# Slots of single columns, two light degrees ranked last, and a reordered attention setup in a graph-and-experts kernel

## What is computed

```
x = x + gat(layernorm(x), src, dst, W, att_src, att_dst, bias)        # attention over each node's incoming edges, 8 heads
x = x + experts(layernorm(x))                                         # each node goes through one of 32 experts, 256 -> 64 -> 256
x = x + relations(layernorm(x), weight[16], edge_weight, edge_type)   # out[dst] += (x[src] @ weight[type]) * edge_weight
x = x + two_experts(layernorm(x))                                     # two of 8 experts, the same two for all nodes, 256 -> 512 -> 256
```

## Time and profile before

| | us |
|---|---|
| median of three runs | 3556.42 (3555.38 to 3558.89) |
| the profiled execution | 3553.55 |
| its span | 3551.9 |
| busy PE / DVE / POOL / ACT | 2038.9 / 1808.5 / 1954.4 / 757.0 |
| stages, from the trace: search and ranking | 0 to 293.8 |
| attention, experts, relation products | 293.8 to 2012.6 |
| relations | 2012.6 to about 3078 |
| choose two, feed-forward | 3078 to 3551.9 |

### The profile page before, as it was taken

How to read it: one execution, slowest core, us unless ns; L and a number is a source line. 1 busy time by engine, 2 the same in 40 slices (tenths; PEclk the granted TensorE clock), 3 DMA queues, 4 the chain that set the end, 5 groups by cost and what they waited for, 6 DMA issues and landing times. The chain is left out here.

```text
span 3551.9 us, 37123 instructions
## 1 busy us (share of the span) xinstructions
PE 2038.9 (57%) x7510; PEld 1302.1 (37%) x7510; DVE 1808.5 (51%) x4035; ACT 757.0 (21%) x1428; POOL 1954.4 (55%) x1920
## 2 busy tenths in 40 slices
PE   1600399999999999999979500000000000369996
PEld 1400266565666656666546200000000000346664
DVE  7643765555556666566530254544454444314545
ACT  3200133333333333333223200000000000013331
POOL 5434874455655767777710277777777777300111
PEclk9955699999999999999989855555555555579998
DMA  6536344445555555554522533333333333100000
GB/s 237 212 102 179 86 126 136 142 135 155 144 146 152 146 166 149 168 165 143 150 87 76 173 106 106 105 106 105 106 105 105 105 105 105 45 30 12 18 18 25
DMA packets 209182, 416.09 MB, mean 117 GB/s; under 512 B 53562, under 2 KB 96018, under 8 KB 208930
## 3 DMA queue, kind: packets, MB, share of 16 engines
q0 software_dynamic: 87168, 239.28, 25.3%
q1 hardware_dynamic: 114706, 167.99, 13.3%
q10 hardware_dynamic: 7056, 6.63, 0.5%
HBM read 259.06 MB, written 154.68 MB: 116 GB/s over the span
## 5 line engine op out<-in xcount | busy, mean ns | idle before, releaser
L822 POOL DMA_INDIRECT gat_rows<-h_table,gat_idx x824 | 923.2, 1120 | 468.8 <-issue 246.0
L1412 POOL DMA_INDIRECT rel_rows<-transformed,rel_idx x824 | 779.1, 945 | 258.2 <-issue 258.2
L1042 PE MATMUL bank<-tr_wr,tr_xt 128*128 128x512 f32 x1568 | 725.1, 602 | 33.8 <-ACT tr_row L913 28.9
L1584 PE MATMUL bank<-weight,rec 128*128 128x1 f32 x196 | 42.0, 352 | 1073.0 <-DVE weight L1610 1073.0
L1584 PEld LDWEIGHTS bank<-weight,rec 128*128 128x128 f32 x196 | 41.9, 333 | 1073.8 <-DVE weight L1610 1073.8
L1009 PE MATMUL bank<-mo_xt,mo_w 128*128 128x256 f32 (+1 forms) x1600 | 429.1, 392 | 1.6 <-ACT mo_ones L894 1.6
L1487 DVE SCALAR_TENSOR_TENSOR bank<-rel_rows,rel_now,bank 128x256 f32<-128x256 f32 x823 | 403.1, 490 | 51.6 <-DVE bank L1487 27.0
L1042 PEld LDWEIGHTS bank<-tr_wr,tr_xt 128*128 128x128 f32 x1568 | 294.4, 192 | 322.9 <-issue 276.4
L913 ACT ACTIVATE tr_row<-bank 128x512 f32<-128x512 f32 x392 | 233.7, 597 | 678.1 <-PE bank L1042 665.5
L1027 PE MATMUL bank<-mo_w,mo_ht 128*128 128x256 f32 x1568 | 366.7, 380 | 0.0
L1009 PEld LDWEIGHTS bank<-mo_xt,mo_w 128*128 128x128 f32 x1600 | 286.3, 192 | 133.0 <-issue 101.2
(11 more groups left out here) (274 smaller groups left out, 2034.7 us busy)
## 6 DMA issues: line engine op xcount, KB each, us to landing
transformed<-tr_row SPq DMA_DIRECT2D x392, 256.0 KB, 2.4
windows<-win SPq DMA_DIRECT2D x34, 736.0 KB, 3.2
gat_rows<-h_table,gat_idx POOLq DMA_INDIRECT x824
rel_rows<-transformed,rel_idx POOLq DMA_INDIRECT x824, 2.8
h_table<-hrow ACTq DMA_DIRECT2D x49, 132.0 KB, 2.1
xa<-x SPq DMA_DIRECT2D x1, 6272.0 KB, 23.9
rec<-x_moved SPq DMA_DIRECT2D x1, 6272.0 KB
tr_x<-records SPq DMA_DIRECT2D x24, 256.0 KB, 4.1
```

Source lines behind the costliest of these rows:

```text
L822: pool.indirect_dma_start(out=rows[:, column(u, j), :], out_offset=None, in_=p.h_table[:], in_offset=bass.IndirectOffsetOnAxis(ap=idx[u][: ...
L1042: ins = pe.matmul(p.bank[6 + c % 2][:], xt2[:, k, u * P:(u + 1) * P], wr[:, k, m * CW:(m + 1) * CW], start=(k == 0), stop=(k == KD - 1))
L1412: pool.indirect_dma_start(out=rows[b][:, j, :], out_offset=None, in_=p.transformed[:], in_offset=bass.IndirectOffsetOnAxis(ap=idx[b][:, j: ...
```

## The change

There are four parts. (1) Ranking: the bins are no longer min(degree, 63). Degrees 0 to 8 keep their bins, degrees 9 and 10 get bins 62 and 63, and all above move down by two, so the order of the nodes is rising in degree but for those with 9 and 10, which come last. DVE computes that with four small operations instead of one. (2) `COLS1` is 8 columns and then 1 at a time: 25 slots instead of 13. The same code computes the counts from it (the shift becomes one by 0 bits). (3) ScalarE clears `rows` instead of DVE, with a copy scaled by 0; POOL waits for it (`cleared`) behind `tables`, and DVE waits for it before its tile loop. (4) In DVE's setup the block of windows and `tables` stands ahead of the fill of `score`, the masks and the expert setup with its wait for `set_turned`.

```diff
-COLS1 = [8] + [2] * (WIN // 2 - 4)
+COLS1 = [8] + [1] * (WIN - 8)
+LAST_DEGREES = N_EDGES // N_NODES * 5 // 8 - 1, N_EDGES // N_NODES * 5 // 8
...
-            chain(dve.tensor_scalar(bin_[:], xa[:, :, C_DEG], float(DBINS - 1), None, ALU.min))
+            lo_last, hi_last = LAST_DEGREES
+            apart = hi_last - lo_last + 1
+            chain(dve.tensor_scalar(bin_[:], xa[:, :, C_DEG], float(lo_last), float(DBINS - 1 - hi_last), ALU.is_ge, ALU.mult))
+            chain(dve.scalar_tensor_tensor(bin_[:], xa[:, :, C_DEG], float(DBINS - 1), bin_[:], ALU.min, ALU.add))
+            chain(dve.tensor_scalar(rank[:], xa[:, :, C_DEG], float(hi_last + 1), float(hi_last + 1 - DBINS - apart), ALU.is_ge, ALU.mult))
+            chain(dve.tensor_tensor(bin_[:], bin_[:], rank[:], ALU.add))
...
             pool.wait_ge(tables, 1)
+            pool.wait_ge(cleared, 1)
...
         @block.scalar
         def _(act):
+            act.activation(rows[:], p.ones[:, 0:1].unsqueeze(2).broadcast_to([P, WIDTH, HT]), ACT.Copy, scale=0.0).then_inc(cleared, 1)
             act.wait_ge(tables, 1)
...
             chain(dve.tensor_copy(p.tails[:], row[:, 2, :]))
-            chain(dve.memset(rows[:], 0.0))
-            chain(dve.memset(score[:], LOWEST))
-            chain(dve.tensor_copy(identb[:], p.ident[:]))
-            dve.tensor_scalar(other[:], spread(p.ident[0:E0, 0:E0], 2, [E0, E0, H0]), BIG, None, ALU.mult).then_inc(other_ready, 1)
-            dve.wait_ge(set_turned, 1)
-            chain(dve.tensor_copy(rwt[:].rearrange("q k e -> q (k e)"), p.bank[2][:, 0:KD * E0]))
-            dve.tensor_copy(b1[:], p.bank[3][:, 0:BLOCKS]).then_inc(set_ready, 1)
-
             for u in range(2):
                 dve.wait_ge(wins_in[u], 16)
...
             dve.sem_inc(tables, 1)
+            chain(dve.memset(score[:], LOWEST))
+            chain(dve.tensor_copy(identb[:], p.ident[:]))
+            dve.tensor_scalar(other[:], spread(p.ident[0:E0, 0:E0], 2, [E0, E0, H0]), BIG, None, ALU.mult).then_inc(other_ready, 1)
+            dve.wait_ge(set_turned, 1)
+            chain(dve.tensor_copy(rwt[:].rearrange("q k e -> q (k e)"), p.bank[2][:, 0:KD * E0]))
+            dve.tensor_copy(b1[:], p.bank[3][:, 0:BLOCKS]).then_inc(set_ready, 1)
+
+            dve.wait_ge(cleared, 1)
             dve.wait_ge(placed, 1)
```

More of the change, by code:

```diff
@@ L666, in attention @@
         rw, b1_rows = xn[0:E0, 0, :], xn[0:BLOCKS, 1, 0:P]
-        bias_in, start_ready = (p.sem(x) for x in ("gat_bias_in", "gat_start_ready"))
+        bias_in, start_ready, cleared = (p.sem(x) for x in ("gat_bias_in", "gat_start_ready", "gat_cleared"))
         wins_in = [p.sem(f"gat_wins_in{u}") for u in range(2)]
```

## The result

| | before, us | after, us |
|---|---|---|
| median of the runs | 3555.9 (3554.27 to 3558.89, 4 runs) | 3527.11 (3523.52 to 3532.56, 4 runs) |
| the profiled execution | 3553.55 | 3532.56 |
| its span | 3551.9 | 3530.6 |

The ratio is 0.9921, with a 95% interval of 0.9906 to 0.9935: 28.8 us by the medians. The profiled execution of after is the slowest of its four, so the two profiles are only 21.0 us apart and the two spans 21.3.

A forecast was written before the change was run, and what follows sets the result against it. PE bounds most of attention, except its start and the heavy tiles at its end, and POOL's gathers bound the relations. +0.7 - 8 + 2.0 - 20.9 = -26.2 from 3553.55 gives 3527.3, plus 2.9 for the median: 3530 us, range 3515 to 3545.

The forecast's parts named there:

- ranking: Before attention: three small DVE instructions added ahead of the one-hot, on the path to POOL's scatter; +0.7 us, between 0 and 1.5.
- head: Attention's setup: first window gather 12.8 us earlier, less 3.8 for three more columns and 1 for slots; -8 us (-12 to 0).
- heavy tiles meeting PE: End of attention: 18 more columns from tile 35 to 46 move PE's 21.9 us stall one group forward; +2.0 us (-8 to +10).
- relations, gathers: Relations stage, bound by POOL: 15 gathers fewer at 1.25 us each, if POOL stays without gaps; -18.8 us.
- relations, end behind POOL: After POOL's last gather: DVE, late with heavy tile 46, finishes tile 48 at T + 19.9 instead of 22.0 us behind; gains 2.1.
- more tests of slots: POOL's branches at slot ends: 466 instead of 265 in each stage, hidden by gathers already queued; cost taken as nothing.
- feed-forward: The feed-forward stage does not see the change; no time gained or lost.
- 3.8 for columns and 1 for slots: Attention up to PE's second and third groups: 79 columns instead of 76 cost 3.8 us, third slots in tiles 6 to 8 cost 1.
- the rival of the loaded DMA: Attention's start: first gathers run beside the relation weight loads, tile 0's rows or SP's record load slip; 3538 us, chance 0.16.
- the rival of crowded columns: End of attention: 18 columns at 1.5 us (+4.5), tile 46's second half waiting for tile 45's sum (+5); 3540 us, chance 0.12.
- The rival that put the kernel above before: POOL's added slot-end branches no longer hidden, 0.30 us each: +60 us in relations, about 15 in attention; 3605 us, chance 0.05.

The follow-up runs named there:

- the kernel with every column a slot: Changed kernel with each of the first eight columns its own slot too, 809 columns in the same order; 3527.9 us, ratio 0.9924 to the kernel before.
- single columns alone: Kernel before with only COLS1 changed to single columns from the ninth on, 799 columns; ratios to before 0.9877 and 0.9856, on two chips with pauses.
- the kernel without ranking: Changed kernel with its ranking taken back to rising degree, 799 columns; ratios to the kernel before 0.9832 and 0.9821, on two chips with pauses.
- another order with six columns fewer: Changed kernel with tiles of degree 22 and above ranked behind degree 13, then 14 to 21 rising, 803 columns; 3510.1 us, ratio 0.9870 to before.

## Why the prediction was right

Forecast 3530.0, measured 3527.1. That the two are only 3 us apart is partly luck. Between the profiles the gain is 21.3 us where the sum had 26.2, and between the medians 28.8; the steps missed by up to 3.3 us each, in both directions. By the prediction's steps, between the two profiles:

| step | predicted, us | measured, us |
|---|---|---|
| ranking | +0.7 | +0.6 |
| head | -8 | -10.7 |
| heavy tiles meeting PE | +2.0 | +5.3 |
| relations, gathers | -18.8 | -16.1 |
| relations, end behind POOL | -2.1 | -1.4 |
| more tests of slots | 0 | 0 (12 ns each at most) |
| feed-forward | 0 | +1.0 |
| sum | -26.2 | -21.3 (spans) |

**Ranking.** The stage starts at 294.4 instead of 293.8. One pair of traces can't tell that from nothing: the stage's first gather stands at 294.92 and 296.38 us in two executions of the kernel before. The feed-forward's +1.0 is of the same kind: it takes 474.8 to 476.0 us in the traces without pauses, whatever the kernel.

**Head.** The clearing took 10.92 us (11.1 estimated from the 5.32 of rows 5), and the window gather came at 308.21 (308.8). Part of that fit is luck. The prediction had the tables last, at 305.7, with the unexplained idle time of 2.75 us before the old memset moved to the windows. It did not move there: DVE does the windows from 301.31 to 303.49 without a gap, and POOL waited for the clearing, which ended at 305.30.

With the stage's start taken off, the head start is 14.0 us at the gathers and 10.7 at PE. The 3.3 us between are nearly the 3.8 for columns and 1 for slots that had been counted, but they were lost in another place. The first gathers issued at an unbroken 1.25 us beside the weight transfers; the rule that was cited for it (the Trainium skill, "DMA: Bandwidth & Descriptors", section "SWDGE vs HWDGE vs iDMA": each engine round-robins between the kinds of queues) agrees with that. But tile 0's rows landed late: its score is 5.1 us behind the end of its last gather, where it was 2.7 in before, and SP's first load of records went from 324.65 to 330.53. So at tile 0's score the head start is down to 11.6 us. In tiles 1 to 3 DVE does not wait for gathers in either kernel, and at tile 6's score the head start is still 11.6: the three columns that were counted at 3.8 us cost nothing up to there. The step that was wrong is therefore the count of columns; in its place stands 2.4 us of the rival of the loaded DMA, which did reach PE.

**Heavy tiles.** Right in place and form: one stall of 20.8 us at the turn that needs tile 46, PE's 63 us behind it, the light tiles without effect. The turn comes 9.6 us behind the score (10.2 predicted). What was mis-sized is the score itself: 1723.6, where 1730.2 less the actual head start of 10.1 is 1720.1. The 3.5 us between are within what executions differ by: with the same columns in the same order, the kernel with every column a slot has this score 4.6 us earlier (behind the stage's first gather). So the +5.3 of the table is one execution's, and the rival of crowded columns is neither needed nor excluded by it. That the prediction counted columns from tile 35 on was nearly right: POOL's last waits for sums stand at tile 36 in before and in tile 37 in after, apart from one of 1.83 us in each, and from there on a column costs PE time. Those columns took about 1.58 us each on average (366.7 us for 232 in before, 335.8 for 214 in after), beside DVE's sums; at that average 18 columns would be 28.4 us, where the prediction had 26.1.

The row that the prediction kept against the Trainium skill can be read closer. In the trace of before, at a sum of a tile of 18 columns:

```profile
1349.68 2.00 POOL L822 DMA_INDIRECT gat_rows<-h_table,gat_idx  x1 [0.30 <-issue]
1351.98 1.99 POOL L822 DMA_INDIRECT gat_rows<-h_table,gat_idx  x1 [0.30 <-issue]
1354.28 2.01 POOL L822 DMA_INDIRECT gat_rows<-h_table,gat_idx  x1 [0.30 <-issue]
...
1348.47 1.22 DVE L1240 TENSOR_TENSOR gat_rows<-gat_rows 128x1024 f32<-128x1024 f32 x1
...
1350.78 1.22 DVE L1240 TENSOR_TENSOR gat_rows<-gat_rows 128x1024 f32<-128x1024 f32 x1
...
1353.08 1.22 DVE L1240 TENSOR_TENSOR gat_rows<-gat_rows 128x1024 f32<-128x1024 f32 x1
```

Between two weighings (L1240) stands one addition (L1249, 1.25 us). The weighings end at 1349.69, 1352.00 and 1354.30, and the gathers start at 1349.68, 1351.98 and 1354.28: one gather for each two DVE operations with both inputs in SBUF, 2.00 us long instead of 0.95. The Trainium skill, "SBUF — State Buffer", section "Who interferes with whom", says that such an operation contends with GpSimd's reads; the trace agrees with that sentence, if an indirect gather reads its row numbers there, which no run here separates. It does not agree with the inference that descriptor generation goes on unhindered.

**Relations.** 15 gathers fewer, and nothing else changed. That the gain is 16.1 and not 18.8 us is the profiled execution's own: its cadence is 1.2530 us instead of 1.2498, and 809 times 3.3 ns are 2.6 us. The same two values come with one and the same kernel: single columns alone has a mean gather of 945 ns in one execution and 948 in the other, the kernel without ranking 948 and 945. It follows neither the columns nor the tests.

**End.** Tile 46 was done 3.0 us before POOL's end, as worked out; tiles 47 and 48 took 0.7 us more than counted. Light tiles behind a heavy one save little, because DVE is still at the heavy one.

**Tests.** The rival that put the kernel above before (exposed branches, decided at 0.13 us) fell clearly. The page that gives about 108 ns for a compare and branch ("Advanced Engine Details and Errata", "Control Flow Timing", in the Trainium skill) may be right about one alone; no run here shows a test alone. Between these gathers it costs about a ninth of that at most, and in the relations' idle time nothing is seen of it.

**What the total hides.** The ranking adds ten columns and puts the heavy ones where PE waits for them. On a chip with pauses the kernel is 74 us slower with it than without. On a chip without them the kernel without ranking never ran, so the 22 to 25 us expected of leaving it out are not shown; what was measured there is another order with six columns fewer, 17 us faster.

## What to carry to other kernels

Before one sorts work so that light pieces come last, ask for each consumer how fast it can take them: a light tile gives back only what lies above the consumer's own time (63 us here), and in both stages the heavy tile before it was still in the way. Count a saved unit only where its engine is the bound; in a stage with two bounds, look in the trace for the last wait of the feeding engine ahead of the stall, and count from there. Before a difference of a few us between two traces is explained, look how far two executions of one program differ in that stage. And a kernel whose bound engine hides everything on one chip may be bound by a chain on another; parts that cost nothing here can take the whole gain there.

## What was not expected of the hardware

- Two of three chips stopped POOL once for every two tiles of the relations, for 12.2 and 11.4 us on average (23 pauses in one kernel, 5.8 to 18.0 us), with gathers of unchanged 945 to 948 ns between them. The whole kernel took 4384 and 4386 us instead of 3555. Twelve of the 23 end 0.6 to 1.2 us behind a packet of the instruction queue; the cause is open.
- The duration of the relations' gathers comes in two values, 945 and 948 ns, by the execution, both of them on one and the same chip too.
- A kernel with a ranking moved 251 or 252 packets through its instruction queue, one without 236 to 238, whatever its columns. What of the ranking causes that is open.
- 128x12864 elements of 4 bytes were cleared by ScalarE in 10.92 us, and by DVE in 10.78: moving it cost nothing and freed DVE.
